# Sparse rows of the first four tiles of a recommender kernel: fetched row by row from ScalarE's queue in place of gathers from GpSimd

## What is computed

```python
other_info = concat([dense] + [emb_sparse[i][sparse_inputs[:, i]] for i in range(3)])
seq_embed  = concat([emb_seq[i][seq_inputs[:, :, i]] for i in range(2)])      # 2048 x 40 x 128
item_embed = concat([emb_seq[i][item_inputs[:, i]] for i in range(2)])
info = concat([q, seq_embed, q - seq_embed, q * seq_embed])                   # q: item_embed for each step
h = sigmoid(info @ att_W1 + att_b1); h = sigmoid(h @ att_W2 + att_b2)
logits = where(mask, h @ att_Wf + att_bf, NEG_INF)
user_info = einsum('bl,bld->bd', softmax(logits), seq_embed)
info_all = batchnorm(concat([user_info, item_embed, other_info]))
# then prelu(@ ffn_W1), prelu(@ ffn_W2), sigmoid(@ out_W)
```

## Time and profile before

| | |
|---|---|
| Median of 3 runs | 1719.14 us (1718.82 to 1720.24) |
| Span of the profiled execution, first to last instruction | 1718.7 us, 0.4 us under the median |
| GpSimd busy | 1285.4 us, 75% of the span |
| TensorE, VectorE, ScalarE busy | 956.0, 476.8 and 421.1 us |
| Gathers: history, sparse, item | 1280, 48 and 32 |
| Last history gather issued; last sparse gather issued | at 1642.78 and 1703.67 us |

### The profile page before, as it was taken

The page is one execution under the profiler, slowest core; times in us unless marked ns, Lnnn a source line. Parts: engine busy times, 40 slices in busy tenths (PEclk is TensorE's granted clock), DMA queues, the critical chain, the costliest instruction groups (busy, mean ns, idle before and its releaser), DMA issues.

```text
span 1718.7 us, 11717 instructions
## 1 busy us (share of the span) xinstructions
PE 956.0 (56%) x2832; PEld 439.9 (26%) x2832; DVE 476.8 (28%) x1351; ACT 421.1 (24%) x770; POOL 1285.4 (75%) x1364
## 2 busy tenths in 40 slices
PE   1554656546564555646556464654646555464567
PEld 0222322222222222222222222322223222222222
DVE  1141322414133141322314132141322314132242
ACT  1131232213222131222213123221222213122222
POOL 6777777777777777777777777777777777777775
PEclk9656666566666656666566666656666565666655
DMA  3111111111111111111111111111111111111122
GB/s 50 28 26 26 27 27 27 26 26 27 27 27 26 26 27 26 27 26 26 27 26 27 26 26 27 26 27 26 26 27 26 27 26 27 27 26 27 26 26 19
DMA packets 56142, 46.22 MB, mean 27 GB/s; under 512 B 34209, under 2 KB 34337, under 8 KB 56097
## 3 DMA queue, kind: packets, MB, share of 16 engines
q0 software_dynamic: 43520, 44.65, 14.9%
q1 hardware_dynamic: 12578, 1.18, 0.5%
HBM read 45.74 MB, written 0.01 MB: 27 GB/s over the span
## 4 chain that ended last, share of the span: by engine, by line
POOL 54%; issue 26%; DMA 18%; POOLq 0%; PE 0%; DVE 0%; ACT 0%; SPq 0%; DVEq 0%; ACTq 0%
POOL hist L268 50%; DMA hist<-in_L_rec_emb_seq_dram,idx 18%; POOL sparse_rows L268 3%; POOL items L268 2%; DMA sparse_rows<-in_L_rec_emb_sparse_dram,idx_sparse 0%; POOLq L289 0%; DMA raw<-in_r_item_inputs_dram 0%; POOLq L60 0%; PE pre L410 0%; POOLq L288 0%; PE pre L416 0%; PE pre L411 0%; PE logits L422 0%; ACT x_sparse L446 0%; POOLq L271 0%
## 5 line engine op out<-in xcount | busy, mean ns | idle before, releaser
L268 POOL DMA_INDIRECT hist<-in_L_rec_emb_seq_dram,idx x1280 | 1208.7, 944 | 390.1 <-issue 351.1
L319 PE MATMUL turned<-ident,hist 128*128 128x128 f32 x640 | 176.0, 431 | 479.8 <-POOLq L289 424.1
L632 DVE TENSOR_TENSOR prod_t<-turned,item_t 128x512 f32<-128x512 f32 x160 | 110.6, 691 | 772.3 <-ACT hist_t L457 772.3
L325 PE MATMUL pre<-hist_t,w_hist 128*80 128x512 f32 x320 | 296.0, 1026 | 32.4 <-ACT hist_t L457 32.4
L319 PEld LDWEIGHTS turned<-ident,hist 128*128 128x128 f32 x640 | 122.7, 227 | 556.6 <-POOLq L289 474.0
L327 PE MATMUL pre<-prod_t,w_raw 128*80 128x512 f32 x320 | 255.1, 894 | 0.0
L457 ACT COPY hist_t<-turned 128x512 f32<-128x512 f32 x160 | 93.7, 586 | 567.8 <-PE turned L319 567.8
L462 ACT ACTIVATE hidden<-pre 80x512 f32<-80x512 f32 x160 | 94.6, 591 | 422.5 <-DVE pre L640 422.5
L640 DVE TENSOR_TENSOR pre<-pre,item_part 80x512 f32<-80x512 f32 x160 | 111.2, 695 | 236.0 <-PE pre L327 236.0
L687 DVE SCALAR_TENSOR_TENSOR sums<-hist,weight,sums 128x128 f32<-128x128 f32 x576 | 156.6, 347 | 0.0
L341 PEld LDWEIGHTS logits<-wf,hidden 128*128 128x128 f32 x640 | 110.3, 227 | 161.6 <-ACT hidden L467 92.7
(11 more groups left out here) (91 smaller groups left out, 416.2 us busy)
## 6 DMA issues: line engine op xcount, KB each, us to landing
hist<-in_L_rec_emb_seq_dram,idx POOLq DMA_INDIRECT x1280, 2.4
sparse_rows<-in_L_rec_emb_sparse_dram,idx_sparse POOLq DMA_INDIRECT x48, 3.3
raw<-in_r_seq_inputs_dram SPq DMA_DIRECT2D x1, 600.0 KB, 5.1
items<-in_L_rec_emb_seq_dram,idx POOLq DMA_INDIRECT x32, 3.4
w_raw<-in_L_rec_att_W_dram SPq DMA_DIRECT2D x1, 160.0 KB
fw<-in_L_rec_ffn_W_dram SPq DMA_DIRECT2D x3, 40.0 KB
ident<-identity_dram SPq DMA_DIRECT2D x1, 64.0 KB, 1.8
dense_rows<-in_r_dense_inputs_dram SPq DMA_DIRECT2D x1, 64.0 KB
```

The lines of the kernel that those rows point to most:

```text
L268: gp.indirect_dma_start(rows, None, table, bass.IndirectOffsetOnAxis(ap=index, axis=0)).then_inc(landed, 16)
L319: last = nc.tensor.transpose(turned[g % 2][:, j * P:(j + 1) * P], hist[:, half, step * D:(step + 1) * D], ident[:, :])
L325: nc.tensor.matmul(pre1[g % 2][0:A1, :], w1_hist[:, :], hist_t[:, g % 2, :], start=True, stop=False)
L632: nc.vector.tensor_tensor(prod_t[:, slot, :].rearrange("p (l b) -> p l b", b=P), turned[slot][:, :].rearrange("p (l b) -> p l b", b=P), it ...
```

## The change

GpSimd leaves out the 12 sparse gathers of tiles 0 to 3 (pairs 0 and 1); it keeps the 36 of tiles 4 to 15. The rows of these four tiles (4 x 3 x 128 = 1536 rows of 256 bytes) are now fetched by ScalarE with plain DMAs of one row each. `fetch_lane(lane)` loads the 12 row numbers of one partition (a "lane") from SBUF into registers, four to a load, and issues 12 DMAs from the table to a new buffer in DRAM, `landing`. It is called eight times in each tile: after `sigmoid1` of groups 0 to 5, 7 and 8. So 16 tiles x 8 calls fetch 128 lanes. At the end SyncE waits for the rows of a pair and copies them from `landing` to `sparse_rows` with one DMA; the wait of `turn_sparse` counts 16 for these two pairs. ScalarE waits for `sparse_idx_ready` once before its loop.

```diff
+    ROW_PAIRS = 2
+    ROW_TILES = 2 * ROW_PAIRS
+    BATCH = 4
+    LANES = 8
+    landing = nc.dram_tensor("sparse_landing", (P, ROW_TILES * NS, 2, E), F32).ap()
...
+                for p in range(ROW_PAIRS):
+                    sp.wait_ge(rows_fetched[p], 16 * P * 2 * NS)
+                    sp.dma_start(sparse_rows[:, 2 * p:2 * p + 2, :].rearrange("p t (n h e) -> p (t n) h e", n=NS, h=2),
+                                 landing[:, 2 * NS * p:2 * NS * (p + 1), :, 0:HALF]).then_inc(sparse_landed[p], 16)
...
-            for tile in range(TILES):
+            for tile in range(ROW_TILES, TILES):
...
-                pe.wait_ge(sparse_landed[p], 2 * 16 * NS)
+                pe.wait_ge(sparse_landed[p], 16 if p < ROW_PAIRS else 2 * 16 * NS)
...
+            act.wait_ge(sparse_idx_ready, 1)
+            taken = [act.alloc_register(f"row_number{i}") for i in range(BATCH)]
+            def fetch_lane(lane):
+                    for first in range(0, ROW_TILES * NS, BATCH):
+                        act.load(taken, bass.at_runtime_partition(numbers[:, first:first + BATCH], lane))
+                        for i in range(BATCH):
+                            row = act.snap(taken[i], min_val=0, max_val=NS * V - 1)
+                            slot = first + i
+                            act.dma_start(landing[bass.ds(lane, 1), slot, :, 0:HALF], halves[bass.ds(row, 1), :, :])\
+                                .then_inc(rows_fetched[slot // (2 * NS)], 16)
...
                     sigmoid1(0, 0)
+                    fetch_lane(tile * LANES)
                     copy_group(2, 0)
                     sigmoid1(1, 1)
+                    fetch_lane(tile * LANES + 1)
...
                             sigmoid1(g, s)
+                            fetch_lane(tile * LANES + (step * 2 + (2 + s)))
...
                     sigmoid1(EARLY, 1)
+                    fetch_lane(tile * LANES + 6)
                     sigmoid2(EARLY)
                     copy_group(EARLY + 1, 0)
                     sigmoid1(EARLY + 1, 0)
+                    fetch_lane(tile * LANES + 7)
```

More of the change, by code:

```diff
@@ L49, in build @@
     UP = 64
-    assert D == P and A2 <= UP and TILES % 2 == 0 and GROUPS % 2 == 0 and EARLY == 7 and GROUPS == 10
+    ROW_PAIRS = 2
+    ROW_TILES = 2 * ROW_PAIRS
+    HALF = E // 2
+    BATCH = 4
+    LANES = 8
+    assert TILES * LANES == P and D == P and A2 <= UP and TILES % 2 == 0 and GROUPS % 2 == 0 and EARLY == 7 and GROUPS == 10
+    landing = nc.dram_tensor("sparse_landing", (P, ROW_TILES * NS, 2, E), F32).ap()
     seq_table = emb_seq.rearrange("n v e -> (n v) e")
@@ L198, in build @@
         sparse_idx_ready = sem("sparse_idx_ready")
+        rows_fetched = [sem(f"rows_fetched{p}") for p in range(ROW_PAIRS)]
         sparse_turned = sem("sparse_turned")
@@ L256, in _ @@
                 sp.dma_start(ow[:, :], out_w).then_inc(ffn_weights_loaded, 16)
+            with nc.allow_non_contiguous_dma(reason="two halves of a row"):
+                for p in range(ROW_PAIRS):
+                    sp.wait_ge(rows_fetched[p], 16 * P * 2 * NS)
+                    sp.dma_start(sparse_rows[:, 2 * p:2 * p + 2, :].rearrange("p t (n h e) -> p (t n) h e", n=NS, h=2),
+                                 landing[:, 2 * NS * p:2 * NS * (p + 1), :, 0:HALF]).then_inc(sparse_landed[p], 16)
             sp.wait_ge(score_ready, PAIRS)
@@ L447, in normalised @@
                                             bias=bn_shift[0:k, c:c + 1])
+            act.wait_ge(sparse_idx_ready, 1)
+            taken = [act.alloc_register(f"row_number{i}") for i in range(BATCH)]
+            halves = sparse_table.rearrange("v (h e) -> v h e", h=2)
+            numbers = idx_sparse[0:1, :, :].rearrange("p t n -> p (t n)")
+            def fetch_lane(lane):
+                with nc.allow_non_contiguous_dma(reason="two halves of a row"):
+                    lane = act.snap(lane, min_val=0, max_val=P - 1)
+                    for first in range(0, ROW_TILES * NS, BATCH):
[5 more added lines that the diff above has]
+                                .then_inc(rows_fetched[slot // (2 * NS)], 16)
             with act.Fori(0, PAIRS) as pair:
```

## The result

The changed kernel takes 2839.17 us (median of 4 runs, 2837.48 to 2839.79), the kernel before 1719.34 in the same measurement. The ratio is 1.651 (95% interval 1.6486 to 1.6533). Forecast were 1929 us and a range up to 2200. Slower was right, the size was not.

The account below looks back on a forecast made before the run. ScalarE's chain was to bound the tiles: 60.3 us plus eight calls of 6.9 (55.2) made 115.5 a tile. Start at 33.5, sixteen tiles (1848) and the last network's 48.0 gave 1929 us, 12% slower; range 1716 to 2200.

Parts of the forecast that it names:

- What bounds the kernel: Before the change, GpSimd's gathers: 1.25 us each, 1360 of them, with 82 setting a tile's 102.40 us.
- the 7.5 us: Gain at the kernel's end if additions were free: 15.0 us less on GpSimd, cut to 7.5 by the last network's compute.
- The price of a DMA: In each fetch_lane call on ScalarE: 0.34 us, 0.38 with its register step, 4.6 for twelve; bounds 3.6 and 6.1.
- The price of a load: In each fetch_lane call on ScalarE: 0.75 us for four registers, 2.3 for three loads, between 0.6 and 3.8.
- F: Price of one fetch_lane call on ScalarE: 6.9 us, between 4.2 and 9.9.
- The tile's own part: ScalarE's chain through one tile, without the eight fetch_lane calls: 60.3 us.
- The sum: Whole kernel: tile 0 starts at 33.5, sixteen tiles of 115.5 us, last network 48.0: 1929 us.
- GpSimd hidden: In the tiles, ScalarE's chain bounds; GpSimd idles before a tile's first gather, its 36 sparse gathers done long before the end.
- No change, F from 3.0 to 5.3: Rival, 10%: GpSimd still bounds tiles, the last ends 3F - 5.4 later; sum 1711.2 + 3F - 5.4, within 0.2%.
- Faster: Rival, 5%: ScalarE's queue takes DMAs in far less than SyncE's, F under 3.0; under 1714.8 us, 1711.2 at best.
- Instruction fetch: Rival, 15%: each of 24 jumps back in ScalarE's program waits 2.4 us for code, 58 us more: 1987 us.
- F over 9 us: Rival, 10%: DMAs and loads in ScalarE's calls both near their high ends; 2200 us and more.

Follow-up runs that it names:

- free calls: The changed kernel without any call of fetch_lane, pairs 0 and 1 getting fixed rows from one load at the start: 1713.19 us, ratio 0.9966.
- the cheap form: The changed kernel with each row fetched from DRAM to two partitions of SBUF, SyncE carrying them by way of DRAM to their place: 2053.65 us.

## Why the prediction was wrong, point by point

**What bounds the kernel, and the 7.5 us.** Right. With free calls 6.1 us came between the medians and 7.3 us in the span; pair 7 started at 1699.65 (1699.5 worked out), and the last network of the changed kernel took 48.5 us (48.0).

**The price of a DMA, the step that failed.** It stands in the prediction as "A two-part row is nearest to the 8 partitions: 0.34", with 0.38 for a DMA and its register step and 0.51 as the upper bound. Measured: 0.83 from one DMA to the next. Of the 0.45 us, 0.30 are the DMA, 0.60 against 0.30, by its form; 0.15 are register steps, three to a DMA (0.06, 0.03, 0.03 and the gaps) and not one. For a call that is 12 x 0.45 = 5.4 us. The bound was too low because the rows picked for it all had one form. The trace of before had others in the same queue, which I passed over:

```profile
6.01 1.83 SPq L244 DMA_DIRECT2D raw<-in_r_item_inputs_dram  x1
...
7.89 2.44 SPq L245 DMA_DIRECT2D raw_sparse<-in_r_sparse_inputs_dram  x1
...
22.73 0.59 SPq L251 DMA_DIRECT2D bn<-in_L_rec_bn_gamma_dram  x1
```

The first two go to 128 partitions in 15 and 16 short pieces each, the third in one piece to 64 partitions. None is from DRAM to DRAM, so none gives the price that was needed, but all are above the 0.43 us on which the 0.51 rested, and the first two move 15 and 24 KB, less than others that took 0.43. So size was not what set the price.

**The price of a load.** 0.75 taken, 0.76 measured for two of the three loads of a call and 0.48 for the first. But this agreement is luck: it was worked out from another kind of instruction, and a load of four registers takes 0.32 us with rows to one partition of SBUF and 0.53 in the cheap form, one of three registers 1.03 us. By the Trainium skill (DMA: Bandwidth & Descriptors, Latency and other measured facts) the floor is about 600 ns; the 0.32 us of the run with rows to one partition lie under it, and so do the 0.48 and 0.53. Not in the sum at all was that on ScalarE the first DMA behind a load takes 0.5 us more, 1.5 us a call. Together: 4.6 + 5.4 + 2.0 + 1.5 = 13.5, measured 13.59. F was 6.7 us short, and 128 x 6.7 = 858 us.

**The tile's own part.** 60.3 worked out; from the span, (2836.8 - 33.5 - 48.0 - 128 x 13.59) / 16 = 63.5. The same sum for the other runs above the bound gives 62.0 (rows to one partition), 62.9 (without loads), 62.8 (half the rows) and 62.8 (the cheap form), at calls from 7.5 to 10 us. So the form of the forecast, one constant and 128 F, holds over five kernels; the constant was 3 us a tile too small, 51 us in all. Where they are: behind call 6 the tile shown takes 1529.50 - 1515.91 = 13.6 us to the end of sigmoid1, against 11.6, and from the last copy to the end 18.5 against 16.8. TensorE's matmuls are longer there: four of layer 2, from 1517.38, in 1.12 us, where those from 1624.89 took 0.65 before. Its granted clock in the two stretches is 0.50, so the lower level, 1.2 GHz, all the time, behind waits of over 10 us for ScalarE; before it was 0.63 and 0.60. The wait for code (below) is in this part too, 17.1 us and so 1.1 us a tile, which the prediction had as a rival. Steps of the inner loop are even 0.3 us shorter than I had.

**The sum.** 1929 + 858 + 51 = 2838, against a span of 2836.8.

**GpSimd hidden.** Right: its waits are on `tile_consumed` and `idx_ready`, and its last sparse gather starts at 2591 us, 197 us before pair 0.

**No change, F from 3.0 to 5.3.** The rival's mechanism was right, though not this kernel's case: with calls of 4.18 us GpSimd set the tiles, and the time was 1721.48 us, 0.1% over the kernel before. Its form gives 1713.2 + 7.1 = 1720.3.

**Faster.** The mechanism asked for a queue on ScalarE that is quicker than SyncE's. The two take the same for a call, 13.6 us. (Even "0.26 at the least" was not the least: SyncE's store of the scores took 0.24 us before.) The Trainium skill's sentence (DMA: Bandwidth & Descriptors, Issuing engines are not separate DMA queues), that what starting a DMA takes of a sequencer is "usually small relative to the DMA itself", is no guide here: a row's DMA takes 0.83 us of the queue with its register steps, a third of the 2.4 us in which a gather lands, and where 12 gathers took GpSimd 15 us, the 1536 DMAs with their loads take ScalarE 1740 us. No run shows how long a row's DMA itself takes to land.

**Instruction fetch.** It is there, at a third of my price. ScalarE is idle for 17.1 us, 7 times, 2.44 us on average, and always at the jump back of the loop over pairs. That this is a wait for code is inferred, but well: two instruction DMAs of 8 KB run in the 2.44 us shown above, the page's instruction DMAs go from 41 to 102, and the run without calls, with its short loop, has 41 of them and no such wait. None of the 16 jumps of the inner loop shows one; the calls on both sides of it are alike. So the rule of the Trainium skill (Runtime: NRT & Kernel Launch, Instruction fetch mechanics) (a taken branch to a page that is not held stalls) agrees with what the long body shows, and 2.4 us was the right price, but for 7 jumps and not 24.

**The chances.** "F over 9 us" had 10% and is what happened, but not as it was described: it wanted DMAs and loads near their high ends, and the loads were in the middle of theirs while the DMA lay beyond its end, 0.83 against 0.51. With 0.51 and 1.28 as ends its own upper end was still 9.9; the cause lay outside all that the range was made of.

## What to carry to other kernels

A price for an instruction is good only for its form: before a row of the trace is used for an added DMA, see that source, destination and pieces are the same, look at every row of that queue and not at the nearest ones only, and if no row has that form, leave the range open by a factor and not by the spread of the rows at hand. Engines that look idle can have their slack in a serial stretch; here 15% busy was the bound, and the sum of one tile's chain, piece by piece, with the added piece as an unknown, told the break-even at once. Work for a queue goes to the engine that has nothing behind it: the same calls cost 1120 us on ScalarE and 112 us on SyncE, and, halved, they bring 6 us there.

## What the runs showed of the hardware that I had not expected

- Issuing a DMA of one row took 0.22 to 0.34 us between DRAM and SBUF with one piece to each of one to eight partitions, and 0.52 to 0.71 us from DRAM to DRAM, from SBUF to SBUF, or with 2 or 16 pieces in one partition. ScalarE and SyncE agree. A register in the address made no DMA longer, from DRAM to DRAM or to one or two partitions of SBUF; its register steps come on top.
- Loading four registers from SBUF took 0.32, 0.53 and 0.76 us on ScalarE, in kernels that differ in the form of the DMAs between the loads; in the changed kernel it took 0.48 us where no DMA stood right ahead; three registers took 1.03 us. The first DMA behind a load took up to 0.5 us more on ScalarE (1.09 against 0.60; 0.48 against 0.25 in the cheap form), and no more on SyncE (0.63 to 0.67 against 0.62) or with rows to one partition (0.55). The cause is open.
- A jump back over a loop body of some 470 rows cost ScalarE 2.44 us of idle time on average, 7 times, with instruction DMAs under way in it.
